# Order tables of a two-layer attention kernel: the six gelu tiles of a pass in one run with no score tile among them

## The chip, the cores and the metric

The kernel runs on one core of a Trainium2 chip. The metric is the device time of one execution in microseconds (us). The times of before are three runs: 2160.82, 2161.02 and 2162.99 us. Names of engines: PE is TensorE's matmuls and PEld its weight loads, DVE is VectorE, ACT is ScalarE, POOL is GpSimd, SP is SyncE, which here only issues DMAs.

## The reference, cut to what matters

Sixteen images of 196 patches and 128 text tokens go through two layers of 324 tokens and 192 channels. Everything is float32.

```python
h = tok(x, L0_tok_W);  h = concatenate([h, txt], axis=1)
h = h + L0_attn(layernorm(h))        # softmax over tokens, then a circular convolution
h = h + L0_ffn(layernorm(h))         # gelu(x @ in_weight.T + in_bias) @ out_weight, 768 hidden
h = h + L1_attn(layernorm(h))        # 12 heads, 324 own keys + 196 shared keys, softmax
h = h + L1_ffn(layernorm(h))         # experts: top_k picks, 12-head softmax attention and gelu MLP of 768, then w2
```

The change concerns three of these computations: the gelu of `L0_ffn` (`jax.nn.gelu(..., approximate=False)` of 768 hidden channels), the gelu of the same size in `L1_ffn`, and the softmax exponentials of the two 12-head attentions, which are computed between them.

## The kernel before

One program does sixteen images in two loops. The first loop (`one`, tables `ORDER_1` and `OFF_1`) does everything up to and with the attention of the shared keys, the second (`two`, `ORDER_2` and `OFF_2`) the expert layer. A pass `i` of a loop works on several images at once, each stage some passes ahead or behind by the offset of its step (`hid` 1, `norm` -1, and so on). Around the middle the last passes of the first loop and the first of the second are woven together (`woven`). Of the 16 passes of each loop in which `hid` does its work, all but one have it beside scores of the same loop: in the first loop passes 0 to 14, in the second passes 0 to 14, of which the first is woven. In the second loop passes 6 to 13 are a hardware loop whose waits are against registers, passes 1 to 5 and 14 are written out.

The order of the work is written by hand. Each string of a table is a slot, each word an item, and every engine walks the same list in the same order, doing of each item what is its own. There is no scheduler. The words that matter here:

- `s`: one score tile. PE multiplies into one of two banks of `sps` (line 1370), ACT takes the exponential into `prob` (line 943). Product n waits until the exponential n-2 has read its bank. In the text they are score n and exponential n.
- `m`: one tile for the row maxima. PE multiplies into one of three banks of `mps` (line 1400), DVE reduces it (line 1228).
- `a`: PE sums `prob` times values for one slot of four heads (line 1385) and waits for each of the four exponentials. In the first loop the `a` of slot 3 takes exponentials 8 to 11; eleven `s` stand ahead of slot 3, so exponential 11 is that of slot 3's first `s`.
- `hid0` to `hid5`: PE fills one of two banks of `lin` (line 1356, two matmuls, of which the trace records four), ACT takes the gelu into `g` (line 843). `hid2` waits until the gelu of `hid0` has read its bank, and so on.
- `norm`: DVE multiplies the attention's result by reciprocal sums (line 1075). `proj4`: PE's projection of it (line 1337), which needs `norm`.
- `pack1`, `tload`: DMAs that SP issues. `pack1` fetches the next keys and queries of four heads (lines 614 and 617), `tload` fetches `gm8` and `hxb` for the final sum (lines 703 and 704). `hold` is a copy on POOL, `end` the final sum on DVE (lines 1275 and 1278) and the store.
- `p` is a step of the expert picks on DVE in some passes; `r` transposes the row maxima.

The exponential and the gelu use different function tables of ACT. Where one follows the other in ACT's order, the program has an `ACT_TABLE_LOAD` ahead of the activation. In the written-out passes of the second loop a wait for the filled bank stands on the load ahead of `hid0`'s gelu; in the hardware loop and in the first loop the load carries none.

Of the kernel before, what the change touches and what calls it, by code (L numbers as in the profile page):

```python
# [36 lines left out]
    "a ln2_1 m m m s v_0.0 s ln2_2 ln2_3 s s m v_0.1 m s m p v_1.0 s recip s",  # L37
    "t2_0 m a m s t2_1 m m s",
    "m s a s m hid0 m hid1 pack2",
    "m hid2 shared hid3 s m s m hid4 m m p norm a m",  # L40
    "hid5 m m s s m proj4_0.0 m den m proj4_0.1 s spread0 spread1 proj4_1 s s ln4_0 a s hx ln4_1 r ln4_2 s",
    "out_0.0 m m out_0.1 a m p out_0.2 m ln4_3 out_0.3 m out_1.0 m out_1.1",
    "s m s ln3_0 tok.0 s tok.1 m m m s hab t4_0 t4_1 ln3_1 s m hb m a m log m s t5_0",
    "exp p m ln3_2 s s ln3_3 t5_1 s m m s a",
# [18 lines left out]
    "out_0.2 m s m out_0.3 s s pack0 a",  # L63
    "r p out_1.0 s out_1.1 s s a",
    "fin_0.0 s s m a s s p m",
    "fin_0.1 s s a m s s m fin_1.0 s m s p m m s hold end hid0 hid1 pack1 m m m s tload hid2 p m m",
    "a hid3 r hid4 hid5",
)
OFF_2 = {"den": -1, "recip": -1, "spread": -1, "norm": -1, "fin": -1, "end": -1, "v": 0, "out": 0, "pack2": 0,
# [1565 lines left out]
```

## Time and profile before

| | us |
|---|---|
| median of three runs | 2161.02 |
| lowest, highest | 2160.82, 2162.99 |
| profiled execution | 2163.17 |
| its span, first to last instruction | 2161.4 |
| PE busy | 1898.0 (88% of the span) |
| DVE busy | 1425.0 (66%) |
| ACT busy | 1119.6 (52%) |
| POOL busy | 267.0 (12%) |

The first loop's passes take about 82 us each and lie at 140 to 1300 us of the span; the woven part follows; the second loop's passes take 41 to 43 us and lie at 1550 to 2140 us. PE is the engine that is busy nearly all the time, so a row matters by what PE waits for. A row of the timeline gives start, length, engine, line, operation, result and operands, a count of merged instructions, and in brackets the idle time before it with what ended that.

### The profile page before, as it was taken

How to read it: one execution, taken by the hardware profiler on the slowest of the kernel's cores; microseconds unless marked ns; L12 is line 12 of the kernel's file. 1: busy time of each engine (PE TensorE's matmuls, PEld its weight loads, DVE VectorE, ACT ScalarE, POOL GpSimd, SP SyncE). 2: the span in 40 equal slices, each digit the busy share in tenths (PEclk: the TensorE clock that was granted, in tenths of full speed). 3: DMA queues.
4: the chain of work that ended last, by engine and by line, in shares of the span. 5: the costliest groups of instructions: out<-in, count | busy, mean ns of one | idle time of the engine just before them, and what ended most of it. 6: DMA issues, size and time to landing. Idle time of an engine off the chain costs nothing. (4 is left out here: it accounts for less than half of the span.)

```text
span 2161.4 us, 42850 instructions
## 1 busy us (share of the span) xinstructions
PE 1898.0 (88%) x11904; PEld 1267.3 (59%) x11904; DVE 1425.0 (66%) x4566; ACT 1119.6 (52%) x2585; POOL 267.0 (12%) x406
## 2 busy tenths in 40 slices
PE   3688998998998998998998987767899999999996
PEld 2465665666665666665665654434566666666664
DVE  3267777767867867868868866524677656566563
ACT  1244554554554554554554554353565656566563
POOL 4301101101101101101101101100011001001000
PEclk9799999999999999999999999978999999999998
DMA  4202112112112112112122021302334333433431
GB/s 150 53 16 55 49 32 61 37 39 60 42 39 56 40 45 57 40 47 57 37 51 57 27 55 51 80 25 68 76 89 114 78 97 94 110 93 89 115 83 35
DMA packets 157452, 134.86 MB, mean 62 GB/s; under 512 B 31924, under 2 KB 136344, under 8 KB 157208
## 3 DMA queue, kind: packets, MB, share of 16 engines
q1 hardware_dynamic: 153592, 127.90, 22.7%
q0 software_dynamic: 2304, 4.79, 0.9%
q8 instruction: 58, 0.95, 0.2%
q10 hardware_dynamic: 1440, 0.75, 0.1%
q14 instruction: 58, 0.48, 0.1%
HBM read 81.96 MB, written 50.16 MB: 61 GB/s over the span
## 5 line engine op out<-in xcount | busy, mean ns | idle before, releaser
L1228 DVE TENSOR_REDUCE mxh<-mps 108x1 f32<-108x260 f32 (+1 forms) x1728 | 684.5, 442 | 351.2 <-PE mps L1400 340.3
L943 ACT ACTIVATE prob<-sps 108x324 f32<-108x324 f32 x1536 | 623.1, 439 | 523.5 <-PE sps L1370 477.6
L1400 PE MATMUL mps<-kpack,qpack 96*108 96x260 bf16 (+1 forms) x1728 | 420.9, 298 | 56.2 <-DMA kpack<-scr_k 25.0
L1370 PE MATMUL sps<-qpack,kpack 128*108 128x324 bf16 x1536 | 440.8, 321 | 33.4 <-ACT prob L943 26.7
L1400 PEld LDWEIGHTS mps<-kpack,qpack 96*108 96x108 bf16 x1728 | 220.5, 131 | 210.4 <-DVE mxh L1228 86.7
L1385 PE MATMUL aps<-prob,v 128*32 128x324 f32 x3072 | 318.5, 459 | 3.7 <-ACT prob L943 1.2
L1370 PEld LDWEIGHTS sps<-qpack,kpack 128*108 128x108 bf16 x1536 | 192.2, 129 | 211.8 <-ACT prob L943 149.9
L1356 PE MATMUL lin<-yT,w 128*128 128x324 f32 x576 | 186.0, 455 | 18.1 <-ACT g L843 13.7
L1356 PEld LDWEIGHTS lin<-yT,w 128*128 128x128 f32 x576 | 103.6, 194 | 63.8 <-issue 32.7
L1385 PEld LDWEIGHTS aps<-prob,v 128*32 128x32 f32 x3072 | 73.2, 110 | 105.2 <-issue 60.3
L758 POOL CAST piece<-rest 128x324 bf16<-128x324 f32 x96 | 43.6, 454 | 729.5 <-DVE rest L1060 721.9
L777 POOL TENSOR_TENSOR hx<-ha,xna 108x576 f32<-108x576 f32 x16 | 22.4, 1397 | 863.2 <-DVE xna L1030 863.2
L1356 PE MATMUL lin<-xT,w_in 128*128 128x324 f32 x384 | 119.8, 445 | 0.5 <-ACT xT L839 0.5
L1346 PE MATMUL lin<-w,g 128*108 128x192 f32 x576 | 108.0, 329 | 2.7 <-PEq L136 2.7
L1346 PE MATMUL lin<-w_out,g 128*108 128x192 f32 x576 | 108.1, 330 | 2.0 <-PEq L136 2.0
L1329 PE MATMUL lin<-ident,xn 108*96 108x108 f32 x384 | 62.2, 284 | 46.3 <-DVE xn L1030 37.5
L957 ACT COPY av<-aps 128x324 f32<-128x324 f32 x96 | 41.1, 428 | 103.2 <-PE aps L1385 78.0
L1346 PEld LDWEIGHTS lin<-w,g 128*108 128x108 f32 x576 | 91.2, 173 | 5.7 <-issue 3.4
L1346 PEld LDWEIGHTS lin<-w_out,g 128*108 128x108 f32 x576 | 92.0, 176 | 4.2 <-issue 2.5
L943 ACT ACT_TABLE_LOAD x65 | 83.4, 1283 | 14.8 <-PE sps L1370 12.9
L843 ACT ACT_TABLE_LOAD x66 | 84.7, 1283 | 8.7 <-PE lin L1356 7.6
L1356 PEld LDWEIGHTS lin<-xT,w_in 128*128 128x128 f32 x384 | 68.0, 193 | 28.2 <-ACT g L843 5.1
(157 smaller groups left out, 2402.4 us busy)
## 6 DMA issues: line engine op xcount, KB each, us to landing
qpack<-scr_q SPq DMA_DIRECT2D x96, 243.0 KB, 3.3
kpack<-scr_k SPq DMA_DIRECT2D x96, 121.5 KB, 3.3
scr_q<-piece SPq DMA_DIRECT2D x32, 243.0 KB, 3.1
scr_k<-piece SPq DMA_DIRECT2D x32, 243.0 KB, 4.0
kpack<-scr_k SPq DMA_DIRECT2D x96, 81.0 KB, 3.1
bc<-rec_d SPq DMA_DIRECT2D x128, 60.8 KB, 2.4
scr_q<-piece SPq DMA_DIRECT2D x32, 162.0 KB, 3.5
scr_q<-piece SPq DMA_DIRECT2D x64, 81.0 KB, 3.4
```

The lines of the kernel that those rows point to most:

```text
L758: nc.gpsimd.tensor_copy(piece[:, m, 1, :], rest[:, m, :]).then_inc(att.second.sem, 1)
L777: nc.gpsimd.tensor_tensor(hx[:, :, :], ha[:, :, :], xna[:, :, :], ALU.add).then_inc(hx_ready.sem, 1)
L843: nc.scalar.activation(g[:, f, :], ring.at(i, what)[:, 0:N], ACT.Gelu, bias=b_in[:, f:f + 1] if bias else 0.0).then_inc(ring.free["act"].s ...
L943: nc.scalar.activation(prob[0:rows, n % NP, :], sps[0:rows, n % 2, 0:N], ACT.Exp, scale=SCALE).then_inc(att.exped.sem, 1)
L957: nc.scalar.copy(av[:, q, :], aps[:, 0:N]).then_inc(att.copied.sem, 1)
L1228: nc.vector.tensor_reduce(mxh[:, hd, t, s:s + 1], att.mps.at(i, use)[0:P, 0:att.width], AX.X, ALU.max, negate=True).then_inc(att.mps.free[ ...
L1329: done = nc.tensor.transpose(b[0:KC, t * P:(t + 1) * P], src[:, t, k * KC:(k + 1) * KC], ident[0:P, 0:P])
L1346: done = mm(tiles2(b)[0:P, t % 2, :], acts[k][:, t * P:(t + 1) * P], weights[k], start=k == 0, stop=k == 5)
L1356: done = mm(b[0:size, 0:N], w[:, k, c:c + size], x[:, k, 0:N], start=k == 0, stop=k == 1)
L1370: mm(sps[0:rows, n % 2, 0:N], kpack[:, 4 * q + n % 4, k * att.rows:k * att.rows + rows], qpack[:, 4 * q + n % 4, :], start=True, stop=True ...
L1385: mm(aps[32 * hd:32 * hd + 32, 0:N], att.values[:, k, 4 * q + hd, :], prob[:, n % NP, :], start=k == 0, stop=k == kt - 1).then_inc(att.sum ...
L1400: mm(bank[0:P, 0:att.width], qpack[0:6 * D, 4 * q + hd, t * P:(t + 1) * P], kpack[0:6 * D, 4 * q + hd, s * att.width:(s + 1) * att.width], ...
```

## The change

Two strings of `ORDER_1` and one of `ORDER_2` are rewritten. No word is added or removed.

```diff
@@ ORDER_1, slots 3 and 4
-    "m hid2 shared hid3 s m s m hid4 m m p norm a m",
-    "hid5 m m s s m proj4_0.0 m den m proj4_0.1 s spread0 spread1 proj4_1 s s ln4_0 a s hx ln4_1 r ln4_2 s",
+    "m hid2 shared hid3 m hid4 m hid5 m s s m p norm a m",
+    "m m s s m proj4_0.0 m den m proj4_0.1 s spread0 spread1 proj4_1 s s ln4_0 a s hx ln4_1 r ln4_2 s",
@@ ORDER_2, slot 7
-    "fin_0.1 s s a m s s m fin_1.0 s m s p m m s hold end hid0 hid1 pack1 m m m s tload hid2 p m m",
+    "fin_0.1 s s a m s s m fin_1.0 s m s p m m s hold end s tload hid0 hid1 pack1 m m m hid2 p m m",
```

In the first loop the two `s` between `hid3` and `hid4` go behind `hid5`, and `hid5` goes ahead of `a`. In the second loop the `s` between `hid1` and `hid2` and the `tload` behind it go ahead of `hid0`.

ACT, first loop, the six gelus (`g`) of one pass and the exponentials (`prob`) about them, the order of before and the order of after in one difference:

```order
 L943 ACTIVATE prob<-sps 108x324 x3
 L843 ACT_TABLE_LOAD
-L843 ACTIVATE g<-lin,b_in 128x324 x4
-L943 ACT_TABLE_LOAD
-L943 ACTIVATE prob<-sps 108x324 x2
-L843 ACT_TABLE_LOAD
-L843 ACTIVATE g<-lin,b_in 128x324 x2
-L943 ACT_TABLE_LOAD
-L943 ACTIVATE prob<-sps 108x324 x3
+L843 ACTIVATE g<-lin,b_in 128x324 x6
+L943 ACT_TABLE_LOAD
+L943 ACTIVATE prob<-sps 108x324 x5
```

Two of the pass's four loads are gone, and the exponentials 11 and 12 stand behind the sixth gelu. In the second loop ACT's order changes in the same way. Counted over all passes, 30 passes have two loads less.

PE, first loop, from `hid2` and `hid3` on to the product ahead of `proj4`, before:

```order
L1356 MATMUL lin<-xT,w_in 128x324 x4
L1370 MATMUL sps<-qpack,kpack 108x324
L1400 MATMUL mps<-kpack,qpack 108x260
L1370 MATMUL sps<-qpack,kpack 108x324
L1400 MATMUL mps<-kpack,qpack 108x260
L1356 MATMUL lin<-xT,w_in 128x324 x2
L1400 MATMUL mps<-kpack,qpack 108x260 x2
L1385 MATMUL aps<-prob,v 32x324 x4
L1400 MATMUL mps<-kpack,qpack 108x260
L1356 MATMUL lin<-xT,w_in 128x324 x2
L1400 MATMUL mps<-kpack,qpack 108x260 x2
L1370 MATMUL sps<-qpack,kpack 108x324 x2
```

The same place after:

```order
L1356 MATMUL lin<-xT,w_in 128x324 x4
L1400 MATMUL mps<-kpack,qpack 108x260
L1356 MATMUL lin<-xT,w_in 128x324 x2
L1400 MATMUL mps<-kpack,qpack 108x260
L1356 MATMUL lin<-xT,w_in 128x324 x2
L1400 MATMUL mps<-kpack,qpack 108x260
L1370 MATMUL sps<-qpack,kpack 108x324 x2
L1400 MATMUL mps<-kpack,qpack 108x260
L1385 MATMUL aps<-prob,v 32x324 x4
L1400 MATMUL mps<-kpack,qpack 108x260 x3
L1370 MATMUL sps<-qpack,kpack 108x324 x2
```

Between score 11 and the sums `a` stood a hidden tile and four small products before; now one score and one maxima product do.

PE, second loop, the place of `hid0` to `hid2` (the rows of four and two are `hid0` with `hid1`, and `hid2`), in one difference:

```order
 L1400 MATMUL mps<-kpack,qpack 108x324 x2
-L1370 MATMUL sps<-qpack,kpack 108x324
+L1370 MATMUL sps<-qpack,kpack 108x324 x2
 L1356 MATMUL lin<-yT,w 128x324 x4
 L1400 MATMUL mps<-kpack,qpack 108x324 x3
-L1370 MATMUL sps<-qpack,kpack 108x324
 L1356 MATMUL lin<-yT,w 128x324 x2
```

Score 35 stands directly behind score 34, ahead of `hid0`. On SP the two DMAs of `tload` (`gm<-gm_d`, `hxb<-hx_d`) stand ahead of the four of `pack1` in place of behind them. The orders of DVE (but for one row in the woven part) and POOL are the same.

## Rows read from the trace of the kernel before

**Rows 1.** Costliest groups of the page: loads of ACT's tables, count, mean ns
```profile
L843 ACT ACT_TABLE_LOAD x66 | 84.7, 1283 | 8.7 <-PE lin L1356 7.6
L943 ACT ACT_TABLE_LOAD x65 | 83.4, 1283 | 14.8 <-PE sps L1370 12.9
```

**Rows 2.** Timeline of a first-loop pass, from `hid0` to behind `proj4`
```profile
547.94 1.25 PE L1356 MATMUL lin<-xT,w_in 128*128 128x324 f32 x4
...
549.15 1.25 PE L1356 MATMUL lin<-xT,w_in 128*128 128x324 f32 x4
...
552.73 0.30 PE L1370 MATMUL sps<-qpack,kpack 128*108 128x324 bf16 x1
...
552.93 0.53 ACT L843 ACTIVATE g<-lin,b_in 128x324 f32<-128x324 f32 x1 [0.56 <-PE lin L1356]
...
553.23 1.25 PE L1356 MATMUL lin<-xT,w_in 128*128 128x324 f32 x4
553.48 1.28 ACT L943 ACT_TABLE_LOAD   x1
...
554.64 1.36 PE L1385 MATMUL aps<-prob,v 128*32 128x324 f32 x8
...
555.26 0.14 PEld L1385 LDWEIGHTS aps<-prob,v 128*32 128x32 f32 x2 [0.47 <-ACT prob L943]
...
557.79 1.14 PE L1337 MATMUL lin<-w_p,av 128*108 128x192 f32 x6
...
559.22 0.77 ACT L943 ACTIVATE prob<-sps 108x324 f32<-108x324 f32 x2
...
559.97 0.30 PE L1370 MATMUL sps<-qpack,kpack 128*108 128x324 bf16 x1
```

**Rows 3.** Timeline, the same pass: sums whose exponentials were all there
```profile
546.97 0.75 PE L1385 MATMUL aps<-prob,v 128*32 128x324 f32 x8
```

**Rows 4.** Timeline of PEld: the wait at `a`, first and last of fifteen passes
```profile
146.53 0.14 PEld L1385 LDWEIGHTS aps<-prob,v 128*32 128x32 f32 x2 [0.47 <-ACT prob L943]
...
1291.76 0.14 PEld L1385 LDWEIGHTS aps<-prob,v 128*32 128x32 f32 x2 [0.47 <-ACT prob L943]
```

**Rows 5.** Timeline of a second-loop pass of the hardware loop, about `hid0` to `hid2`
```profile
1854.11 1.31 ACT L943 ACTIVATE prob<-sps 108x324 f32<-108x324 f32 x3 [0.62 <-PE sps L1370]
...
1854.60 0.12 PEld L1370 LDWEIGHTS sps<-qpack,kpack 128*108 128x108 bf16 x1 [0.28 <-ACT prob L943]
...
1854.78 2.35 PE L1356 MATMUL lin<-yT,w 128*128 128x324 f32 x8
1855.44 1.28 ACT L843 ACT_TABLE_LOAD   x1
...
1857.52 1.25 PE L1356 MATMUL lin<-yT,w 128*128 128x324 f32 x4
```

**Rows 6.** Timeline of a written-out second-loop pass: load ahead of `hid0`'s gelu, and `hid2`
```profile
1598.98 1.28 ACT L843 ACT_TABLE_LOAD   x1 [0.69 <-PE lin L1356]
...
1600.86 1.33 PE L1356 MATMUL lin<-yT,w 128*128 128x324 f32 x4 [0.32 <-ACT g L843]
```

**Rows 7.** Timeline, hardware-loop pass: SP's queue, and the products that need `pack1`
```profile
1858.10 1.38 SPq L617 DMA_DIRECT2D kpack<-scr_k  x3
...
1859.67 0.92 SPq L703 DMA_DIRECT2D gm<-gm_d  x1
1860.78 0.40 SPq L704 DMA_DIRECT2D hxb<-hx_d  x1
...
1864.26 0.31 PEld L1400 LDWEIGHTS mps<-kpack,qpack 96*108 96x108 bf16 x3 [0.52 <-issue]
```

**Rows 8.** DMA issues of the page: `kpack`, last number us from issue to landing
```profile
kpack<-scr_k SPq DMA_DIRECT2D x96, 81.0 KB, 3.1
```

**Rows 9.** Waits, whole span: PE for `kpack`'s DMA (us in total, times, longest)
```profile
PE mps L1400 <- DMA kpack<-scr_k: 25.0, 23, 4.3
```

**Rows 10.** Busy time by stretch, first loop: ..., ACT busy, POOL busy, granted clock, DMA
```profile
140.00:1300.00 1160.00, 1050.47 (x6858) 713.23 (x6857) 865.93 (x2986) 616.78 (x1456) 147.01 (x234) 0.98 0.18 46
```

## The prediction, made before the run

> **What bounds the kernel now.** I read the busy times first: PE is busy for 1050 of 1160 us in the first loop, ACT for 617 [rows 10]. So time that ACT saves counts only where PE waits for ACT. Next, the costliest groups: ACT loads a function table 66 + 65 = 131 times, at 1.283 us [rows 1], which is 168 us of ACT. Then the timeline about the gelu tiles of one pass of each loop, to see which of these loads PE waits for. In a first-loop pass PE waits once for an exponential behind a load: the last two of the eight matmuls of the sums `a` start at 555.26 with 0.47 idle before them [rows 2]. That wait is 0.47 in each of the fifteen passes that have scores among the gelus [rows 4]; the passes repeat each other, so one pass times its count is a fair sum.
>
> **What the change removes.** Thirty passes lose two loads each: 60 x 1.283 = 77 us of ACT's busy time, 131 loads become 71. What of it was on PE's path? In the first loop the removed pair is the one that ends at the exponentials 11 and 12 and the one behind it that returns to the gelu. The last pair of the pass is moved, not removed. In before, exponentials 13 and 14 run at 559.22, late because of a load; PE goes on with `proj4` at 557.79 and takes score 15 at 559.97 with no idle noted [rows 2], since exponential 13 has read its bank at about 559.22 + 0.44 = 559.66. So that lateness costs PE nothing, and removing it gives nothing. What PE can win in this stretch is the wait at `a`, about 0.6 us a pass, if exponential 11 came early. It does not.
>
> **First loop: the wait at `a` grows.** Sums `a` need exponential 11. The change puts score 11 behind `hid5` and lets only one score and one maxima product stand between the scores and `a`. I replay one pass from the rows [rows 2].
> - Products: four of them (`s m s m`) lie between 552.73 and `hid4` at 553.23, so one takes 0.125 us. A hidden tile and one product together take 549.15 - 547.94 = 1.21.
> - Now the product behind `hid3` is a maxima product, at 552.73 as before. `hid4` starts at 552.85, `hid5` at 554.06, the next product at 554.06 + 1.085 = 555.15.
> - ACT starts `hid3`'s gelu 0.20 behind the start of the product that follows that tile (552.93 against 552.73). So the gelu of `hid5` starts at 555.35. The load follows 0.55 behind a gelu's start (552.93 to 553.48): 555.90. From the load's start to the weight load that waited for exponential 11 it was 555.26 - 553.48 = 1.78. So the wait now ends at 557.68.
> - PE reaches `a` four products behind 555.15, at 555.65, and with the 0.07 more that lay ahead of `a` before, 555.72. It starts the first three heads and waits until 557.68, 1.96 from the start of `a`.
> - Before, that was 555.26 - 554.64 = 0.62. Cross-check: `a` lasts 1.36 there [rows 2] against 0.75 where all exponentials were ready [rows 3], a difference of 0.61.
>
> The rest of PE's work in the stretch is the same, so each pass grows by 1.96 - 0.62 = 1.34 us. What covered the load before was `hid4` and the products around it, which stood between score 11 and `a`; that cover is gone. DVE has `norm` to do at that time in both orders and is done before `proj4` wants it: about 556.3 + 1.2 = 557.5, against a `proj4` that now starts near 559.1. Fifteen passes: 15 x 1.34 = **+20.1 us**.
>
> The Trainium skill (ScalarE: Activation LUTs, What ACT_TABLE_LOAD costs) says a switch costs about 1283 ns of load and about 1380 ns of drain, 2.66 us in all. The trace agrees on the load (1283 ns) and shows no drain: the load starts 0.55 behind a gelu of 0.53, and the weight load that needs the exponential behind it comes 1.78 from the load's start [rows 2]. By the page's drain the exposed wait would be 1.38 longer and the first loop's term 15 x 2.72 = 40.8 us, an estimate from that page; the sum goes by the rows.
>
> **Second loop: score 35 waits for a bank, and so does `hid2`.** Scores 34 and 35 now stand side by side. Score 34 already waits for exponential 32 and starts its weight load at 1854.60 [rows 5]. Exponentials in a row follow each other by (1.31 - 0.44)/2 = 0.435, so score 35 can start 0.435 later, at 1855.035, and the two hidden tiles behind it slip by 0.435.
> - Written-out passes (1 to 5 and 14, six): the load ahead of the gelu of `hid0` waits for the filled bank (0.69 idle before it), and `hid2` waits for that gelu (0.32 idle) [rows 6]. All of it moves with `hid0`: +0.435 each, 2.6 us.
> - Hardware-loop passes (eight): the load does not wait; it starts 0.02 behind exponential 34. With exponential 35 ahead of it, it starts at 1855.88 instead of 1855.44. From load to `hid2` it is 1600.86 - 1598.98 = 1.88 [rows 6], so `hid2` can start at 1857.76, against 1857.52 before [rows 5]: +0.24 each, 1.9 us.
> - The woven pass 0: the same move among more work. Bounds: 0 and +1.3 (one load laid bare), with a gain of the same 1.3 possible since a load goes. I take the written-out pass's 0.4.
>
> Behind `hid2` the chain is maxima products, reductions, transpose, `hid4`, all released by PE, so nothing takes the shift back. The removed loads lay in the shade of that chain. Sum for the second loop: **+4.9 us**.
>
> **SP's queue.** `tload` goes past `pack1`. Its two issues take from 1859.67 to 1861.18, so `pack1`'s last DMA starts about 1.7 later than the 1859.02 of before: 1860.7. With 3.1 to land [rows 8] it is there at 1863.8; PE wants it at 1864.26 [rows 7] plus the 0.24 of shift. Cost 0, with 0.7 us of room. The two DMAs themselves are needed a pass later. POOL's queue is not touched.
>
> **Sum.** 20.1 + 4.9 = 25.0 us on the profiled execution's 2163.17 gives 2188.2. That execution stands 2.15 above the median of the runs, so the median to expect is 2161.02 + 25.0 = **2186.0 us**, 1.2% slower.
>
> **The rivals.**
> 1. *`pack1` comes too late* (slower still). For: the room is 0.7 us and the 243 KB of `hxb` now go ahead of it. Against: 3.1 us landing is a median of many such transfers. It decides from a landing of 3.8 us. At 4.5 us eight hardware-loop passes lose 0.7 each: +5.6, 2192.
> 2. *The clock falls more often* (slower still). The first loop's mean granted clock is 0.98 [rows 10], so it is at 1.2 GHz for 4% of the time, 46 us, and at 2.4 GHz otherwise. A longer idle time in each pass could add to that. If the mean fell to 0.97, 23 us more would be at the lower level, and at most half of it, 11.6 us, be lost: 2198 at the end, 2190 if a third of that.
> 3. *The delay is taken back later in the pass* (no change, 2157 to 2165). It needs waits of PE that end at a fixed time, whatever PE did before. The nearest are those for `kpack`'s DMA, 25.0 us in all [rows 9], about 0.8 a pass; they alone could not take back 1.34, and the DMAs start from tiles that PE itself made in the same pass. The two loops' growth would have to vanish wholly.
> 4. *Faster: ACT's loads are on the path after all.* The place would be the scores that follow the gelu run: if each removed load had held PE for its 1.28 us, 60 of them would give -77 us and 2084. It decides where PE waits at a score behind a load. The rows show it running into `proj4` and score 15 without idle time [rows 2]. A small form of it, 0.9 us a pass won in thirty passes from a less crowded ACT on top of my sum, would end at 2159, still no gain. The Trainium skill (ScalarE: Activation LUTs, Rules for kernel authors) asks to group by table set and do all of one set before switching; this change follows that rule, and the rule's gain is this rival.
>
> **How the numbers follow.** My forecast as summed 0.66; rival 1 0.12; rival 2 0.15; rival 3 0.04; rival 4 0.03. A measurement of this kernel can tell about 0.2% (4.3 us) from no change. The forecast and rivals 1 and 2 are slower: 0.93. Rival 3 is the same: 0.04. Rival 4 is faster: 0.03. The range: below, the first-loop term could be smaller by 0.3 a pass if PE reaches `a` later than replayed (4.5 us), and the second loop's could be nothing (4.9 us), not likely both: 2179. Above, rival 1 and most of rival 2: 2195.
>
> **What would show it.** In the profile of after: 71 table loads; ACT busy less by some 77 us and PE's span longer; in the first loop one wait of the `a` weight load for `prob` of about 1.8 us in place of 0.47, fifteen times; first-loop passes longer by 1.3 us, hardware-loop passes of the second by 0.2 and written-out ones by 0.4; no wait for `kpack` at the first maxima products of slot 0. I am wrong if the wait at `a` stays near 0.5 us, if the passes keep their length though it grew, or if PE shows a wait for `prob` or `g` that was there before and has gone.

## The result, and the profile after

The changed kernel takes 2192.59 us (median of four runs, 2189.31 to 2200.35) against 2162.01 (four runs, 2160.82 to 2163.4). The ratio is 1.0146, 95% interval 1.0118 to 1.0175: 1.5% slower. The profiled execution took 2190.89 us, its span is 2189.2. In the experiments below, one execution of the kernel with only the first loop changed (6366.22 us) and one of the kernel before beside it (3572.94 us) fell into a far slower state; they are left out of every median and ratio.

The page of after, busy time by engine:

```profile
PE 1919.3 (88%) x11904; PEld 1268.4 (58%) x11904; DVE 1428.7 (65%) x4566; ACT 1045.7 (48%) x2525; POOL 267.3 (12%) x406
```

The groups of after that answer to [rows 1]: table loads, count, busy us, mean ns, and the idle time before them:

```profile
L843 ACT ACT_TABLE_LOAD x36 | 46.2, 1283 | 8.3 <-PE lin L1356 7.9
L943 ACT ACT_TABLE_LOAD x35 | 44.9, 1283 | 14.4 <-PE sps L1370 13.1 <-ACT mT L965 0.9
```

71 loads are left of 131 and ACT is busy for 73.9 us less, yet the span is 27.8 us longer. The waits of the whole span name the place (us in total, times, longest). First the kernel before:

```profile
PEld aps L1385 <- ACT prob L943: 26.9, 80, 1.3
```

and after:

```profile
PEld aps L1385 <- ACT prob L943: 47.3, 82, 1.8
```

The sums `a` wait 20.4 us more for exponentials. The timeline of a pass of the first loop of after, the same as in [rows 2], 5.05 us later in the span:

```profile
552.99 1.25 PE L1356 MATMUL lin<-xT,w_in 128*128 128x324 f32 x4
...
560.30 0.44 PE L1370 MATMUL sps<-qpack,kpack 128*108 128x324 bf16 x2
560.39 0.53 ACT L843 ACTIVATE g<-lin,b_in 128x324 f32<-128x324 f32 x1 [0.67 <-PE lin L1356]
...
560.78 0.75 PE L1385 MATMUL aps<-prob,v 128*32 128x324 f32 x6
560.94 1.28 ACT L943 ACT_TABLE_LOAD   x1
...
562.23 0.77 ACT L943 ACTIVATE prob<-sps 108x324 f32<-108x324 f32 x2
562.72 0.14 PEld L1385 LDWEIGHTS aps<-prob,v 128*32 128x32 f32 x2 [1.79 <-ACT prob L943]
...
563.39 0.54 PE L1400 MATMUL mps<-kpack,qpack 96*108 96x260 bf16 x3
...
563.74 1.43 DVE L1228 TENSOR_REDUCE mxh<-mps 108x1 f32<-108x260 f32 x4 [1.35 <-PE mps L1400]
...
564.22 0.12 PEld L1400 LDWEIGHTS mps<-kpack,qpack 96*108 96x108 bf16 x1 [0.33 <-DVE mxh L1228]
...
564.38 1.16 PE L1337 MATMUL lin<-w_p,av 128*108 128x192 f32 x6
```

Score 11 is issued at 560.30, ACT is still at the sixth gelu, then comes the load (560.94), and exponential 11 starts at 562.23. PE's weight loads have been standing at `a` since 560.93 (562.72 less the 1.79 of idle time). There is also a wait that was not there before: 0.33 at 564.22, for DVE to empty a bank of `mps`. All fifteen passes show the same wait of 1.79 at `a`; the first and the last:

```profile
147.08 0.14 PEld L1385 LDWEIGHTS aps<-prob,v 128*32 128x32 f32 x2 [1.79 <-ACT prob L943]
...
1317.19 0.14 PEld L1385 LDWEIGHTS aps<-prob,v 128*32 128x32 f32 x2 [1.79 <-ACT prob L943]
```

Second loop, a hardware-loop pass of after that answers to [rows 5]:

```profile
1880.54 0.12 PEld L1370 LDWEIGHTS sps<-qpack,kpack 128*108 128x108 bf16 x1 [0.28 <-ACT prob L943]
...
1880.87 0.12 PEld L1370 LDWEIGHTS sps<-qpack,kpack 128*108 128x108 bf16 x1 [0.21 <-ACT prob L943]
...
1881.05 2.35 PE L1356 MATMUL lin<-yT,w 128*128 128x324 f32 x8
...
1881.71 1.28 ACT L843 ACT_TABLE_LOAD   x1
...
1883.65 1.25 PE L1356 MATMUL lin<-yT,w 128*128 128x324 f32 x4
```

Counted from score 34's weight load, `hid0` starts 0.51 later (0.18 before), the load 1.17 (0.84 before) and `hid2` 3.11 (2.92 before). So score 35 costs 0.33, and 0.19 of it is left at `hid2`, because the score that stood ahead of `hid2` is gone from there.

### The profile page after: what moved, and what is told of

It reads as the page before. It is cut to its first block and busy times, and to the rows that moved or that the text cites. A ratio compares the mean times of both kernels' runs of the same rounds, so it can differ in the third digit from the quotient of the medians.

```text
span 2189.2 us, 42790 instructions
## 1 busy us (share of the span) xinstructions
PE 1919.3 (88%) x11904; PEld 1268.4 (58%) x11904; DVE 1428.7 (65%) x4566; ACT 1045.7 (48%) x2525; POOL 267.3 (12%) x406
## 5 line engine op out<-in xcount | busy, mean ns | idle before, releaser
L1385 PE MATMUL aps<-prob,v 128*32 128x324 f32 x3072 | 328.4, 470 | 22.6 <-ACT prob L943 18.7
L1060 DVE TENSOR_TENSOR rest<-lin,piece 128x324 f32<-128x324 f32 x96 | 47.3, 492 | 57.1 <-ACT piece L853 24.8
L1456 PE MATMUL lin<-vz,dft 128*82 128x204 f32 x384 | 78.9, 343 | 1.2 <-PEq L136 1.1
```

Source lines behind the costliest of these rows:

```text
L1060: nc.vector.tensor_tensor(rest[:, m, :], ring.at(i, what)[:, 0:N], piece[:, m, 0, :], ALU.subtract).then_inc(ring.free["dve"].sem, 1)
L1385: mm(aps[32 * hd:32 * hd + 32, 0:N], att.values[:, k, 4 * q + hd, :], prob[:, n % NP, :], start=k == 0, stop=k == kt - 1).then_inc(att.sum ...
L1456: done = mm(b[0:FW, 256 * c:256 * c + C + H], dft[:, t, k, c, :], vz[:, t, :], start=t == 0, stop=t == T - 1)
```

## The experiments

Each differs from the kernel before by the diff shown. Their comparisons are with runs of the kernel before on the same chip: 2159.94 us for the first four, 2160.35 for the next three, 2159.82 for the last three. "The stretch" is the time in a first-loop pass from the maxima product behind `hid0` to the tenth after it, which is in `proj4`. It holds the whole place of the change and repeats within 0.02 us from pass to pass of one kind: 9.73 us before in passes without expert picks and 9.71 with them. In after it is 11.29 and 11.26. Only the first of the fifteen is shorter: 8.95 before and 10.47 after.

**Each loop alone.** The first loop's two strings of the change only:

```diff
-    "m hid2 shared hid3 s m s m hid4 m m p norm a m",
-    "hid5 m m s s m proj4_0.0 m den m proj4_0.1 s spread0 spread1 ...",
+    "m hid2 shared hid3 m hid4 m hid5 m s s m p norm a m",
+    "m m s s m proj4_0.0 m den m proj4_0.1 s spread0 spread1 ...",
```

> Only the first loop's table is changed, the second's is as before. Theory (the wait at the sums a, laid bare fifteen times, is the loss): the stretch from hid0 to proj4 grows by 1.56 us in each of 15 passes, 23 us, and with what the clock takes the median is 2185 to 2192, nearly all of the change's 30 us. Rival (the second loop's table carries a part of it, as the prediction's 4.9 us said): 2184 or less here, and about +5 us in the run with the second table alone.

Measured: 2187.59 us, ratio 1.0117 (1.0089 to 1.0146), that is +25 us (19 to 32); the medians are 28 apart. This is what was expected, 2185 to 2192. The stretch grew by 1.56 us in fourteen of the fifteen passes and by 1.51 in the first, some 23.4 in all.

The second loop's string only:

```diff
-    "... s hold end hid0 hid1 pack1 m m m s tload hid2 p m m",
+    "... s hold end s tload hid0 hid1 pack1 m m m hid2 p m m",
```

> Only the second loop's table is changed. Theory from the trace of after: score 35 costs 0.33 us a pass, and later waits of the same pass (the transpose r on DVE, the keys' DMA) give it back, so the median is within 3 us of before: 2159 to 2165. Rival (the prediction's second term): 15 passes keep 0.2 to 0.4 us each, 2165 to 2167.

Measured: 2164.76 us, ratio 1.0019 (1.0005 to 1.0034), +4.1 us (1 to 7). That is at the upper end of what was expected and just under the rival's range; it does not decide between them. The first loop carries six sevenths of the change, and the two parts add up to what the whole costs, within the intervals.

**Is it the load between score 11 and `a`?** If so, the pair of loads can go without loss when score 11 and its exponential come ahead of the gelus:

```diff
-    "m s a s m hid0 m hid1 pack2",
-    "m hid2 shared hid3 s m s m hid4 m m p norm a m",
-    "hid5 m m s s m proj4_0.0 m den m proj4_0.1 s spread0 spread1 ...",
+    "m s a s m s hid0 m hid1 pack2",
+    "m hid2 shared hid3 m m hid4 m m p norm a m",
+    "hid5 m m s s m proj4_0.0 m den m proj4_0.1 s s spread0 spread1 ...",
```

> First loop: the six gelus in one run as in the change, but score 11 goes ahead of hid0, score 12 behind hid5, and a stands ahead of hid5 as before. Second loop as before. Theory (the loss comes from the load that stands uncovered between score 11 and a, not from the unbroken run): the wait at a is gone, hid2 waits about 0.3 us longer for its bank, each pass is 0.3 us shorter than before, and the median is 2155 to 2161. Rival (a gelu run without scores starves the rest of the pass): 2175 or more.

Measured: 2156.69 us, ratio 0.9986 (0.9971 to 1.0). Its loads are 51 and 50, thirty fewer than before, the same saving in the first loop as the change's. Timeline of PEld in its pass:

```profile
552.08 1.93 PEld L1356 LDWEIGHTS lin<-xT,w_in 128*128 128x128 f32 x8 [0.54 <-ACT g L843]
...
556.00 0.16 PEld L1385 LDWEIGHTS aps<-prob,v 128*32 128x32 f32 x8 [0.19 <-issue]
```

The wait at `a` is gone; all eight weight loads run on. The stretch is 0.68 shorter (0.38 to 0.45 in the passes with picks). About 0.25 of that is only the two scores that left it, at 0.125 each. The rest, about 0.43 in the passes without picks, is the 0.61 that `a` lost to its wait before (1.36 in [rows 2] against 0.75 in [rows 3]) less the 0.19 that `hid2`'s wait grew (0.54, where it is 0.35 in before and in after): exponential 11 now delays the first gelu. So with the same loads removed and the gelus in one run, the loss is gone: neither the run of six nor the missing loads cause it by themselves. This edit also leaves `hid5` behind `a`, as before, so it does not part the wait for exponential 11 from the bunching of the products behind `a`. The rows do: the wait at `a` is 1.79 in each pass where score 11 stands behind the gelus and `hid5` ahead of `a`, and 0.47 before. The next run takes the bunching by itself.

**The bunched maxima products.** The stretch grew by 1.56 and the wait at `a` accounts for 1.32 of it (1.79 less 0.47). The rest should be the three maxima products in a row behind `a`, which fill the three banks. One of them ahead of `a`, otherwise the first loop of the change:

```diff
-    "m hid2 shared hid3 m hid4 m hid5 m s s m p norm a m",
-    "m m s s m proj4_0.0 m den m proj4_0.1 s spread0 spread1 ...",
+    "m hid2 shared hid3 m hid4 m hid5 m s s m m p norm a m",
+    "m s s m proj4_0.0 m den m proj4_0.1 s spread0 spread1 ...",
```

> The change's first table, with one maxima product taken from behind a to ahead of it; second loop as before. Theory (0.2 us of each pass is lost because three products in a row behind a fill the three banks faster than DVE empties them): hid0 to proj4 takes 0.1 to 0.2 us less than in the first table alone, 2 to 3 us in all, and the wait at a stays 1.6 to 1.8 us. Rival (the extra is ACT's or the clock's): no difference to the first table alone in that stretch.

Measured: 2179.33 us, ratio 1.0099 (1.0065 to 1.0133); the stretch grew by 1.21 in place of 1.56, in every pass. Timeline of PEld:

```profile
559.16 0.15 PEld L1385 LDWEIGHTS aps<-prob,v 128*32 128x32 f32 x6 [0.18 <-issue]
560.99 0.14 PEld L1385 LDWEIGHTS aps<-prob,v 128*32 128x32 f32 x2 [1.68 <-ACT prob L943]
561.66 0.17 PEld L1400 LDWEIGHTS mps<-kpack,qpack 96*108 96x108 bf16 x2 [0.53 <-issue]
...
562.07 0.13 PEld L1400 LDWEIGHTS mps<-kpack,qpack 96*108 96x108 bf16 x1
```

The 0.33 wait for DVE is gone (562.07 has none); it had cost the pass some 0.22, as worked out below. And one product of about 0.13 now lies in the shade of the wait at `a`, which shrank from 1.79 to 1.68. Together these are the 0.35. Expected were 0.1 to 0.2: the product that moves into the shade had been left out.

The same step on the version with score 11 ahead, one maxima product moved from behind `hid3` to ahead of `hid2`:

```diff
-    "m hid2 shared hid3 m m hid4 m m p norm a m",
+    "m m hid2 shared hid3 m hid4 m m p norm a m",
```

> The table of the run with score 11 ahead, and one maxima product moved from behind hid3 to ahead of hid2, where PE waits 0.54 us for the gelu of hid0. Second loop as before. Theory (that product fills a wait): each first-loop pass is 0.1 to 0.15 us shorter than with score 11 ahead alone, about 2 us, hid2 waits 0.4 us, and the median is 2152 to 2158. Rival (DVE's reduction or the banks set the pace there): no difference to score 11 ahead alone.

Measured: 2156.34 us, ratio 0.9986 (0.9971 to 1.0001), no difference to the version without it that the runs can tell. The stretch is 0.80 shorter than before against 0.68, and 0.49 to 0.56 against 0.38 to 0.45 in the passes with picks. Both kernels are some 3 us below the kernel before, which is at the edge of what the runs can tell.

**The halves of the second loop's edit.** Score 35 moved alone, `tload` left where it was:

```diff
-    "... s hold end hid0 hid1 pack1 m m m s tload hid2 p m m",
+    "... s hold end s hid0 hid1 pack1 m m m tload hid2 p m m",
```

> Second loop only: score 35 goes ahead of hid0, tload stays behind the maxima products. First loop as before. Theory (the bank that score 35 waits for is what the second table costs): score 35 waits 0.21 us more and hid2 0.15 to 0.5 us in every pass, and the median is 3 to 5 us above before, as with the whole second table. Rival (the two DMAs of tload ahead of pack1 are the cost): within 1.5 us of before.

Measured: 2159.51 us, ratio 0.999 (0.9978 to 1.0002). The theory that score 35 alone costs 3 us or more fell: the interval ends at 0.4 us above before.

`tload` moved alone:

```diff
-    "... s hold end hid0 hid1 pack1 m m m s tload hid2 p m m",
+    "... s hold end tload hid0 hid1 pack1 m m m s hid2 p m m",
```

> Second loop only: tload goes ahead of pack1, score 35 stays between the gelus. Four table loads a pass as before. Theory: the keys arrive 1.7 us later but mostly in time; the first maxima products of slot 0 wait 0.1 us longer in the passes that are written out, and the median is within 1.5 us of before. Rival (late keys): kpack waits at slot 0 in every pass and 3 us or more above before.

Measured: 2159.29 us, ratio 1.0003 (0.9991 to 1.0015), as expected.

Neither half costs anything that the times can tell, and both together cost 4 us. To see whether that holds, the whole second-loop edit, score 35 alone, and the whole change were measured once more beside each other.

> The same table as in the run of the second loop's edit alone, measured once more beside its half. If the +4 us of that run is the edit's own, this one is again 3 to 6 us above the kernel before (ratio 1.0014 to 1.0028). Rival: the edit costs only what the steady rows show, score 35's 0.33 less 0.13 in eight passes, about 1 to 3 us, and the rest of the +4 was scatter of the transfers that the products wait for: then 1 to 3 us (1.0005 to 1.0014).

Measured: 2165.38 us, ratio 1.0012 (0.9999 to 1.0026), that is +2.6 us (-0.2 to 5.6) by the ratio, while the medians are 5.6 apart. The ratio falls to the rival, the medians to the theory: undecided.

> Only score 35 moved ahead of hid0, the two transfers of tload left behind pack1, measured beside the whole edit of the second loop on one chip. If the two halves act together (score 35 delays the products and tload delays their transfer), this one stays within 1.5 us of the kernel before while the whole edit costs 3 to 6. Rival: score 35 alone carries what the whole edit costs, and both come out within 1.5 us of each other.

Measured: 2160.99 us, ratio 1.0003 (0.9992 to 1.0014), +0.6 us (-1.7 to 3.0).

> The whole change once more, on the chip and beside the runs of the two above. By the sum of its parts (first loop alone +25, second alone +1 to +4) it is 26 to 30 us above the kernel before, 2186 to 2190. If it is 31 us or more again, as first measured, something appears only with both tables changed (rival).

Measured: 2194.11 us, ratio 1.0157 (1.013 to 1.0183), that is +34 us (28 to 40), again above 31. By the ratios the parts give 25 + 4 = 29, by the medians 28 + 5 = 33; the intervals are too wide to say that the whole costs more than its parts. Of the second loop: its edit cost 4.1 and 2.6 us in two measurements and half of it -2 and +0.6. By these numbers the whole edit is 2 to 6 us slower than its half, but beside each other on one chip their intervals overlap, so that it is slower at all is not shown, nor what would make it so.

The traces can tell a little more of score 35. In the hardware loop, take the time from `hid0` of pass 6 to `hid0` of pass 13, seven distances. In the kernel with one product ahead of `a`, whose second table is that of before, `hid0` starts there at 1784.31 and 2068.27, in after at 1799.09 and 2085.15. That is 283.96 and 286.06. The other executions with the old table took 284.1, 284.5, 284.8 and 286.2 (before, with 1.6 of waits for `kpack`'s DMA in it); the others with score 35 moved, with or without `tload`, 286.1, 286.3, 286.9, 286.9 and 287.4. The means are 1.9 apart, which is 0.26 a pass. So moving score 35 does cost the hardware-loop passes something, about 2 us over eight, and that is less than the times of one kernel against another can tell. With `tload` alone moved the one profiled execution took 287.2, of which 2.2 were waits for the DMAs of `kpack` and `qpack`.

## Why the prediction was right, and where it was off

The direction, the place and the range were right. The forecast was 2186.0, the time 2192.59, inside 2179 to 2195 and 6.6 above the forecast.

**The wait at `a`.** The replay put the start of `a` at 555.72 and the end of the wait at 557.68. Shifted by the 5.05 us of that pass they are 560.77 and 562.73; the rows of after have 560.78 and 562.72. The gelu of `hid5` was put at 555.35 and the load at 555.90, which are 560.40 and 560.95 after the shift; the rows have 560.39 and 560.94. This worked because every duration in the sum came from a row of the same place. The page of the Trainium skill that the prediction weighed (ScalarE: Activation LUTs, What ACT_TABLE_LOAD costs) would have had a drain of 1380 ns besides the load. No run here shows it: from the gelu's start to the load's it is 0.55, from the load's start to the exponential's 1.29. The rule of the same page of the Trainium skill (Rules for kernel authors), to group by table set, was followed by this change, and the change lost 1.5%. The version with score 11 ahead follows it as well and loses nothing (ratio 0.9986): the rule leaves open what the one remaining load stands in front of.

**The term that was too small.** "The rest of PE's work in the stretch is the same, so each pass grows by 1.34." The work is the same, its spacing is not. From the end of the wait to `proj4` it was 557.79 - 555.26 = 2.53 before [rows 2] and is 564.38 - 562.72 = 1.66 after. With `hid5` gone from there (1.085) it should be 1.44. The other 0.22 goes with the wait for a bank of `mps` at 564.22 (0.33 of idle weight loads, not all of which is lost): `a` used to have `hid5` behind it, during which DVE emptied the banks. So the term is 15 x 1.56 = 23.4, not 20.1, and the run with one product moved ahead shows that the bank wait goes with the bunching.

**The second loop.** The sum of 4.9 agrees with the 4.1 and 2.6 measured, but that is in part luck, for its steps were only partly right: with them corrected the rows give 8 x 0.19 = 1.5 us, and 2 by the seven passes above.
- *Score 35 waits 0.435.* It waits 0.33. I had divided a run of three exponentials, 1.31, by its pitch; but the third of these was late for its own score. Two that have both their scores ready take 0.77, so they are 0.33 apart, and that number stood in [rows 2].
- *Hardware loop +0.24.* It is 0.33 - 0.14 = 0.19. The growth was computed on the wrong wait: `hid2` did not wait for the gelu there, it followed PE's own work, and one score less stands ahead of it. This shift does stay in the pass: the reductions behind it wait for PE's products in both kernels. From score 34's weight load to the first products of slot 0 it is 1864.26 - 1854.60 = 9.66 before [rows 5, 7] and 1890.39 - 1880.54 = 9.85 after:

```profile
1890.39 0.33 PEld L1400 LDWEIGHTS mps<-kpack,qpack 96*108 96x108 bf16 x3 [0.53 <-issue]
```

- *Written-out passes +0.435, nothing takes the shift back.* DVE takes it back. A written-out pass before:

```profile
1683.43 2.35 PE L1356 MATMUL lin<-yT,w 128*128 128x324 f32 x8
...
1685.85 0.76 DVE L1278 TENSOR_TENSOR fin<-fin,hxb 108x576 f32<-108x576 f32 x1
...
1686.53 1.29 DVE L1228 TENSOR_REDUCE mxh<-mps 108x1 f32<-108x324 f32 x3
...
1690.48 0.30 PE L1410 MATMUL mps<-identb,mp 108*12 108x108 bf16 x3 [0.26 <-issue]
...
1693.77 0.31 PEld L1400 LDWEIGHTS mps<-kpack,qpack 96*108 96x108 bf16 x3 [0.53 <-issue]
```

and the same pass after:

```profile
1710.67 2.34 PE L1356 MATMUL lin<-yT,w 128*128 128x324 f32 x8
...
1712.76 0.76 DVE L1278 TENSOR_TENSOR fin<-fin,hxb 108x576 f32<-108x576 f32 x1
...
1713.44 1.29 DVE L1228 TENSOR_REDUCE mxh<-mps 108x1 f32<-108x324 f32 x3
...
1717.41 0.30 PE L1410 MATMUL mps<-identb,mp 108*12 108x108 bf16 x3
...
1720.82 0.31 PEld L1400 LDWEIGHTS mps<-kpack,qpack 96*108 96x108 bf16 x3 [0.64 <-DMA kpack<-scr_k]
```

`hid0` came 27.24 later in the span, but DVE's `end` and the reductions behind it only 26.91, and the transpose `r` 26.93: DVE, busy with `end`, set the time of `r` in both, and PE's 0.33 of shift vanished in it. The chain behind `hid2` is not released by PE alone.

**SP's queue, rival 1.** SP issues `gm` and `hxb` first, and `kpack` later:

```profile
1713.91 0.90 SPq L703 DMA_DIRECT2D gm<-gm_d  x1
1714.86 0.57 SPq L704 DMA_DIRECT2D hxb<-hx_d  x1
...
1715.91 1.38 SPq L617 DMA_DIRECT2D kpack<-scr_k  x3
```

In the written-out pass the first products of slot 0 now wait for `kpack`'s DMA, but by 0.64 against an idle time of 0.53 that was there anyway; they come 27.05 later, 0.12 more than `r`. In the hardware-loop pass they don't wait for it. So the rival is there in its smallest form, some 0.1 in some of the passes, and not the 0.7 of its price; the run with `tload` alone measured no cost in its times.

**The clock, rival 2.** The first loop's mean granted clock did go from 0.98 to 0.97 (stretch, its length, busy time of PE, PEld, DVE, ACT and POOL, then the clock), in after:

```profile
140.00:1310.00 1170.00, 1048.38 (x6774) 703.14 (x6774) 859.21 (x2955) 571.89 (x1410) 147.20 (x234) 0.97 0.17 45
```

But the same happens without the change, and not at the rival's price. The profiled execution in the second measurement of score 35 alone, whose first loop is the one of before, has a lower one still. It took 2166.63 us, 3.5 more than the profiled one of before:

```profile
140.00:1300.00 1160.00, 1065.75 (x6844) 718.82 (x6844) 864.68 (x2977) 618.13 (x1453) 147.28 (x234) 0.96 0.17 46
```

Against [rows 10] it has 0.02 less of granted clock and PE busy for 15 us more. The stretches of the other profiles scatter between 0.96 and 0.98 as well, whatever the table. Over whole executions the mean granted clock was 0.956 with the first loop alone changed against 0.955 before, so the clock does not carry that loop's loss. In the second measurement of the whole change it was 0.952 against 0.956. Among the 21 executions of before beside it, 0.01 less of clock goes with some 5 us more of time, so by this estimate about 2 us of that difference of 34 may be the clock's; that the change lowered it is not shown.

**Rivals 3 and 4** are out: nothing later in the first loop took the 1.56 back, and no wait of the kind of rival 4 was there to win. The gain that the removed loads could give is at most what the version with score 11 ahead shows, about 3 us, at the edge of what can be told from nothing.

**What stays open.** 23.4 for the first loop and 2.6 to 4.1 for the second are 26 to 27.5 of the 30.6 between the medians. The remaining 3 to 5 are within the measurement's interval (25 to 38). The traces hint at the first loop, outside the stretch: from `hid0` of pass 0 to `hid0` of pass 14 the six profiled executions with the old first table took 1141.2 to 1148.5 us (mean 1144.8) and the three with the change's 1170.1, 1172.1 and 1173.4 (mean 1171.9). Of these 27 us the stretch explains 14 x 1.56 = 21.8. But single executions of one table differ by up to 7, and the one with one product ahead of `a` took 1158.3, where its stretch would ask for 1161.7; so this is not shown. The second loop alone scatters by as much between executions of one table. Waits for `kpack`'s DMA from 1530 us on, the kernel before:

```profile
PE mps L1400 <- DMA kpack<-scr_k: 6.0, 9, 1.4
```

and the kernel with only the first loop changed, whose second loop is word for word the same:

```profile
PE mps L1400 <- DMA kpack<-scr_k: 0.8, 2, 0.4
```

## What to carry to other kernels

In this kernel, fewer table loads were worth something only where an engine waited behind one. Before grouping, look up who consumes the first result after the load, and count how much of the consumer's engine's work stands between that result's producer and its use. Grouping activations by table moves the one load that is left; put a result that is needed soon ahead of the group, not behind it: here that, with `hid5` left behind `a`, was the difference between +25 and -3 us in the first loop. When the order of small products changes, count the banks too: the same products bunched behind a wait cost 0.22 us a pass here that they did not cost spread out.

## What the runs showed of the hardware

- A load costs ACT 1.28 us wherever it stands, and an exponential behind it starts 1.29 after the load's start. The change, which removed 60 of them, took 73.9 us off ACT's busy time, and the span grew by 27.8.
- Two exponentials whose scores are ready follow each other by 0.33 (0.77 for two, of 0.44 each), not by the 0.44 that one lasts. A bank is free for the next score at that pace: 1880.87 - 1880.54 = 0.33.
- In executions of one second-loop table, the waits for one kind of DMA went from 0.8 to 6.0 us. One profile of each kernel can't judge an edit worth 4 us of 2160; it took the repeated stretch (0.02 us from pass to pass) in the first loop, and stayed open in the second.
